# The groups of a latent attention, written out sixteen times or looped over two of four batches

## The chip, the cores and the metric

The kernel runs on one core of one Trainium2 chip. The metric is the device time of one execution in microseconds (us), the median of three. Its engines are TensorE (PE, with its weight loads shown as PEld), VectorE (DVE), ScalarE (ACT), GpSimd (POOL) and SyncE (SP, which issues nearly all DMAs here). Each runs its own instruction stream, and they meet only through semaphores.

## What is computed

Two attention layers and a mixture of experts, each with a norm ahead and behind. Only the middle part is touched by the change: an attention of 16 heads whose keys, queries and values have 4 numbers each, over 4 batches of 1024 tokens. Cut to that (B = 4, S = 1024, D = 128):

```python
# first layer: 16 causal heads of 64, tanh projections                    (block 1)
x = x + layernorm(attn_ref(layernorm(x), Wq, bq, Wk, bk, Wv, bv, Wo, bo))
hs = layernorm(x)
# second layer                                                            (block 2)
Q = (hs @ q_w + q_b)  -> [b, 16 heads, s, 8][..., :4]
K = (hs @ k_w + k_b)  -> [b, 16 heads, s, 4];  V = (hs @ v_w + v_b) -> the same
attn = softmax(einsum("bhsk,bhtk->bhst", Q, K) / sqrt(4))
mla_out = concat(einsum("bhst,bhtv->bhsv", attn, V), zeros) @ o_w + o_b
# router, top 2 of 8 experts, expert MLPs, weighted sum                   (block 3)
x = x + layernorm(hs + 0.3 * moe(mla_out))
```

## The kernel before

It is written per engine. Three large blocks follow one another, one for each part above, with a barrier between them. Numbers of the text such as "block 1" mean these.

**Block 1** goes over 32 pairs of heads. Its helper each_pair (lines 392 to 403) writes pairs 0 to 3 out in Python, loops with engine.Fori over pairs 4 to 9 and again over pairs 10 to 29, two pairs in each round, and writes the last two out. Line 396 is the first loop, line 399 the second. In a loop a wait's count is an expression of the loop's variable. **Block 3** loops over the experts in the same manner (line 1760 on TensorE).

**Block 2** is the one at issue. It goes over 16 groups: batch b (4) times gi (4), and a group is four heads of one batch. n = 4 b + gi is its number. A group is 32 items u: half h of the queries, key tile kt (8), pair pr of heads (2). In one item of a group

- TensorE makes the scores of 128 keys by 512 queries for two heads (L1086), then the same kind of product the other way round for a later item, "maxima" (L1116), from which the row maximum is taken 22 items ahead (LEAD), then some small piece of other work ("spare", L1152), and last the values product of two items before (L1101, 8 matmuls);
- ScalarE takes the exponential of the scores (L1293), 128 x 1024;
- VectorE reduces the maxima product to its maximum (L1467), 128 x 1024;
- GpSimd, twice a group, splits the found maxima into three bfloat16 parts (split_tops), which TensorE turns and VectorE puts into the rows of the next queries.

Scores and maxima take turns in three slots of PSUM (SLOT): scores of item u wait for the reduction of the slot's last user, maxima of item u wait for the exponential of item u - 1. Once a batch, at item 13 of gi 3, the order of the slots shifts, and maxima wait for one exponential more (SHIFT_AT, L1231).

In gi 0 and 1 of b 1 to 3 the outputs of the batch before are projected as well. In gi 2 of b 0 to 2 the next batch is prepared: its states are turned (L1067), queries, keys and values projected, split in three parts by GpSimd, and SyncE stores them to DRAM in 24 DMAs (store_part, L999). SyncE's eight loads for the next group (L1013) are issued at each group's start, when the scores of the group before have been issued to the end; TensorE needs them at item 10.

Semaphore counts are ITEMS * n + u + 1 and the like. at_least, prepares and is_first decide what is in a group; of a loop's variable they say "yes, beyond the first", "yes, prepares" and "no". wait_apart (L100) waits and then counts up a semaphore nobody waits for, so that the wait stays an instruction of its own. batch_tiles and the DMA helpers take a symbolic b through bass.ds. each_group (L978) runs group for all 16 on each of five engines, all written out: nothing in block 2 loops.

Of the kernel before, what the change touches and what calls it, by code (L numbers as in the profile page):

```python
# [23 lines left out]
B, S, D = 4, 1024, 128  # L24
# [10 lines left out]
GROUPS = H2 // GH  # L35
N2 = B * GROUPS
# [46 lines left out]
def build(nc, states, Wq, bq, Wk, bk, Wv, bv, Wo, bo, q_w, q_b, k_w, k_b, v_w, v_b, o_w, o_b,  # L83
# [7 lines left out]
    with ExitStack() as ctx:  # L91
# [885 lines left out]

        def each_group(engine, group):  # L978

            for n in range(N2):  # L980
                group(n // GROUPS, n % GROUPS, last=n == N2 - 1)

        def prepares(b):
            return not isinstance(b, int) or b < B - 1
# [1 line left out]
        with nc.Block() as block:  # L986
            @block.sync
            def _(sp):
# [69 lines left out]
                for c in range(PARTS):  # L1058
                    store_part(0, 1, c)
                sp.wait_ge(parts_out, 16 * STORES * 2)  # L1060
                each_group(sp, group)

            @block.tensor
            def _(pe):
# [196 lines left out]
                pe.wait_ge(lv_ready, 1)  # L1261
                turn_tops(0, 0)
                each_group(pe, group)
                values(N2 - 1, 1, ITEMS - 2)
                values(N2 - 1, 1, ITEMS - 1)
# [10 lines left out]
            def _(act):  # L1276
# [70 lines left out]
                for m in range(0, LEAD, 2):  # L1347
                    difference(m, SLOT[m % 3])
                each_group(act, group)
                copy_outputs(N2 - 1, 1)  # L1350
                copy_ao(B - 1, 1)
# [617 lines left out]
```

## Time and profile before

| | |
|---|---|
| three runs | 1759.78, 1766.03, 1773.70 us (median 1766.03) |
| profiled execution | 1773.7 us, span 1772.0 us |
| mean granted TensorE clock | 0.956 of full |
| busy | PE 93%, DVE 81%, ACT 69%, POOL 22% |
| block 1, its 32 pairs | about 50 to 800 us |
| block 2, its 16 groups | about 850 to 1543 us |
| block 3 | about 1545 to 1772 us |

The share of busy time is a mean over these blocks, which have different limits, so it is to be read block by block. Register, branch and semaphore instructions are not counted as busy; the trace has them all the same, as rows with a "q" behind the engine's name. PEclk is the clock that TensorE was granted, as a share of its upper level of 2.4 GHz; 0.5 is the lower level, 1.2 GHz.

### The profile page before, as it was taken

The numbers are of one execution on the slowest core, as the hardware profiler recorded it, in microseconds if no ns is written. First come the engines' busy times: TensorE is split into PE (matmuls) and PEld (weight loads), VectorE is DVE, ScalarE is ACT, GpSimd is POOL, SyncE is SP. The second block draws the span as 40 slices with busy tenths as digits, with TensorE's granted clock in tenths as the row PEclk, the third lists the DMA queues.
The fourth block names the chain that finished last, engine by engine and source line by source line (L and its number), as shares of the span: only waits on it lengthen the run. The fifth ranks groups of instructions, "written<-read, shape, count | busy, mean of one in ns | idle before, by whom it ended". The sixth has DMA issues, their size and how long they took to land. (4 is left out here: it accounts for less than half of the span.)

```text
span 1772.0 us, 38392 instructions
## 1 busy us (share of the span) xinstructions
PE 1640.3 (93%) x14930; PEld 713.5 (40%) x14930; DVE 1438.7 (81%) x2115; ACT 1218.5 (69%) x1185; POOL 384.8 (22%) x506
## 2 busy tenths in 40 slices
PE   2899999999999999985999999999999999889995
PEld 2344444444444444432223233323332332366774
DVE  5377777888888888887898899889989999277888
ACT  3666666666766666642787777777777778756776
POOL 6211112333333333323401000100010212120004
PEclk8999999999999999995899899989999999989998
DMA  4311001100000000002002000200020010000001
GB/s 136 74 48 39 37 37 38 38 37 36 37 37 37 37 26 31 20 4 59 26 26 48 13 13 25 48 14 13 26 48 14 13 37 13 10 6 13 13 12 48
DMA packets 48144, 57.02 MB, mean 32 GB/s; under 512 B 9406, under 2 KB 34462, under 8 KB 48032
## 3 DMA queue, kind: packets, MB, share of 16 engines
q1 hardware_dynamic: 46988, 53.71, 10.1%
q8 instruction: 77, 1.26, 0.3%
q10 hardware_dynamic: 1044, 1.76, 0.3%
q14 instruction: 35, 0.29, 0.1%
HBM read 15.07 MB, written 10.49 MB: 14 GB/s over the span
## 5 line engine op out<-in xcount | busy, mean ns | idle before, releaser
L1293 ACT ACTIVATE arena<-psum 128x1024 f32<-128x1024 f32 x512 | 522.9, 1024 | 152.3 <-PE psum L1086 138.2
L1467 DVE TENSOR_REDUCE arena<-psum 128x2 f32<-128x1024 f32 x490 | 581.4, 1220 | 56.1 <-PE psum L1116 53.0
L652 ACT ACTIVATE arena<-psum 128x2048 f32<-128x2048 f32 (+1 forms) x160 | 273.3, 1708 | 232.7 <-PE psum L537 229.9
L1101 PE MATMUL psum<-arena 128*32 128x256 f32 x4096 | 336.3, 401 | 1.1 <-ACT arena L1307 0.7
L554 PE MATMUL psum<-arena,hs 128*64 128x512 f32 (+3 forms) x1536 | 283.0, 496 | 2.7 <-POOL arena L701 2.2
L701 POOL TENSOR_SCALAR_AFFINE_SELECT arena<-arena 128x512 f32<-128x512 f32 (+1 forms) x160 | 168.0, 1068 | 533.9 <-ACT arena L652 533.9
L1116 PE MATMUL psum<-arena 32*128 32x512 bf16 x1068 | 211.6, 411 | 24.6 <-ACT arena L1346 11.8
L537 PE MATMUL psum<-arena 64*128 64x512 f16 (+3 forms) x2304 | 216.1, 325 | 4.9 <-DVE arena L738 3.6
L1086 PE MATMUL psum<-arena 32*128 32x512 bf16 x1024 | 203.3, 394 | 1.4 <-DVE arena L1489 1.4
L738 DVE TENSOR_TENSOR arena<-arena 128x1024 f16<-128x1024 f32 x64 | 78.4, 1225 | 138.5 <-ACT arena L631 138.5
L554 PEld LDWEIGHTS psum<-arena,hs 128*64 128x64 f32 x1536 | 96.1, 136 | 144.8 <-issue 125.9
L537 PEld LDWEIGHTS psum<-arena 64*128 64x128 f16 x2304 | 96.9, 94 | 137.7 <-issue 57.2
L1086 PEld LDWEIGHTS psum<-arena 32*128 32x128 bf16 x1024 | 48.2, 91 | 220.0 <-issue 135.1
L1101 PEld LDWEIGHTS psum<-arena 128*32 128x32 f32 x4096 | 82.4, 109 | 130.9 <-issue 115.4
L1782 ACT ACTIVATE arena<-psum,b1T 128x1024 f16<-128x1024 f32 x64 | 71.3, 1114 | 49.9 <-PE psum L1691 49.9
L1376 POOL CAST arena<-arena 128x16 bf16<-128x16 f32 x32 | 8.1, 254 | 428.7 <-DVE arena L1482 428.7
L1711 PE MATMUL psum<-arena 128*128 128x128 f16 x1536 | 94.0, 223 | 7.4 <-DVE arena L1624 4.2
L1116 PEld LDWEIGHTS psum<-arena 32*128 32x128 bf16 x1068 | 50.7, 94 | 120.8 <-ACT arena L1293 75.7
L502 PE MATMUL psum<-arena 128*128 128x512 f16 x384 | 95.3, 385 | 3.3 <-ACT arena L631 2.2
L1711 PEld LDWEIGHTS psum<-arena 128*128 128x128 f16 x1536 | 90.9, 100 | 15.6 <-issue 5.6
L1624 DVE TENSOR_TENSOR arena<-arena 128x1024 f16<-128x1024 f32 x60 | 73.1, 1223 | 27.6 <-ACT arena L1783 27.4
L1691 PE MATMUL psum<-arena 128*128 128x512 f16 x384 | 91.3, 389 | 2.2 <-ACT arena L1783 2.2
(202 smaller groups left out, 2122.8 us busy)
## 6 DMA issues: line engine op xcount, KB each, us to landing
arena<-arena SPq DMA_DIRECT2D x32, 512.0 KB, 3.0
arena<-arena SPq DMA_DIRECT2D x48, 128.0 KB, 2.3
arena<-latent_q SPq DMA_DIRECT2D x64, 64.0 KB, 2.0
arena<-latent_k SPq DMA_DIRECT2D x64, 64.0 KB, 2.0
arena<-arena SPq DMA_DIRECT2D x32, 96.0 KB, 2.6
X<-in_L_attn_states SPq DMA_DIRECT2D x4, 512.0 KB, 13.1
arena<-arena SPq DMA_DIRECT2D x32, 64.0 KB, 1.8
out_x<-X SPq DMA_DIRECT2D x4, 512.0 KB, 3.3
```

The lines of the kernel that those rows point to most:

```text
L502: last = nc.tensor.matmul(PJ[:, half * HALF:(half + 1) * HALF], w_qk[par][:, 2 * j + w, :], xT[par][:, x, half * HALF:(half + 1) * HALF], ...
L537: last = nc.tensor.matmul(SC[:, s, c:c + w], k[rows, kt * P:(kt + 1) * P], q[rows, q0:q0 + w], start=(m == 0), stop=(m == 2), skip_group_c ...
L554: last = nc.tensor.matmul(OUT[s * DH:(s + 1) * DH, q0:q0 + w], vals[par][:, kt, s * DH:(s + 1) * DH], probs[g][:, s, c:c + w], start=first ...
L652: nc.scalar.activation(probs[g], SC[:, :, 0:WIDTH[g]], ACT.Exp, scale=DH ** -0.5).then_inc(exp_done, 1)
L701: return nc.gpsimd.affine_select(out=v, in_=v, compare_op=ALU.is_ge, fill=0.0, base=0, pattern=[[0, blocks], [1, P]], channel_multiplier=-1)
L1086: last = nc.tensor.matmul(dst[:, i * HALF:(i + 1) * HALF], k_rows[par][rows, kt * P:(kt + 1) * P], q_rows[par][rows, h * HALF:(h + 1) * HA ...
L1101: last = nc.tensor.matmul(OT[ROWS * c:ROWS * (c + 1), h * HALF // 2:(h + 1) * HALF // 2], v_cols[par][:, kt, 2 * pr + i, :], e_probs[u % 4 ...
L1116: last = nc.tensor.matmul(dst[:, i * HALF:(i + 1) * HALF], q_rows[par][rows, qt * P:(qt + 1) * P], k[rows, :], start=(e == 0), stop=(e == ...
L1293: nc.scalar.activation(e_probs[u % 4], src, ACT.Exp, scale=KD ** -0.5).then_inc(e_done, 1)
L1467: nc.vector.tensor_reduce(half_tops[:, kh, qt, 2 * pr:2 * pr + 2], src.rearrange("p (i c) -> p i c", i=2), AX.X, ALU.max).then_inc(top_don ...
L1691: last = nc.tensor.matmul(HP[c][:, half * HALF:(half + 1) * HALF], w1_e[par][:, w, c * P:(c + 1) * P], mT[:, x, tok], start=(m == 0), stop ...
L1711: last = nc.tensor.matmul(YP[slot][:, tok], h[slot][c][:, tok], w2_e[par][:, w, c, :], start=(c == 0 and m == 0), stop=(c == FC - 1 and m ...
```

## The change

each_group no longer writes all 16 groups out. It writes the four groups of b 0 and of b 3 and loops over b 1 and 2 in between, with the four values of gi written out in the loop's body. The helpers are as they were; they had been written for a symbolic b already. Every engine's stream changes, since all five call each_group.

```diff
         def each_group(engine, group):
 
-            for n in range(N2):
-                group(n // GROUPS, n % GROUPS, last=n == N2 - 1)
+            for gi in range(GROUPS):
+                group(0, gi)
+            with engine.Fori(1, B - 1) as b:
+                for gi in range(GROUPS):
+                    group(b, gi)
+            for gi in range(GROUPS):
+                group(B - 1, gi, last=gi == GROUPS - 1)
```

## Rows read from the trace of the kernel before

**Rows 1.** The page: span, busy time and share, granted clock, the costliest VectorE group.

```profile
span 1772.0 us, 38392 instructions
PE 1640.3 (93%) x14930; PEld 713.5 (40%) x14930; DVE 1438.7 (81%) x2115; ACT 1218.5 (69%) x1185; POOL 384.8 (22%) x506
...
L1467 DVE TENSOR_REDUCE arena<-psum 128x2 f32<-128x1024 f32 x490 | 581.4, 1220 | 56.1 <-PE psum L1116 53.0
```

**Rows 2.** Windows by group: length, busy us of each engine, clock, DMA.

```profile
core 0: us, PE busy (x) PEld busy (x) DVE busy (x) ACT busy (x) POOL busy (x), PEclk, DMA share, GB/s
...
892.40:932.40 40.00, 39.60 (x400) 11.72 (x398) 38.96 (x41) 33.10 (x35) 2.42 (x10) 1.00 0.08 28
...
1157.70:1203.30 45.60, 44.14 (x398) 11.81 (x398) 39.24 (x41) 33.23 (x34) 2.42 (x10) 0.85 0.04 13
1203.30:1246.30 43.00, 41.62 (x414) 13.13 (x414) 40.23 (x42) 33.91 (x36) 2.43 (x10) 1.00 0.05 14
...
1335.40:1378.80 43.40, 41.93 (x398) 11.69 (x398) 39.21 (x41) 33.02 (x34) 2.42 (x10) 0.92 0.04 13
```

**Rows 3.** Timeline, seam of b 1 and b 2: start, length, engine, line.

```profile
1202.21 2.13 ACT L1293 ACTIVATE arena<-psum 128x1024 f32<-128x1024 f32 x2 [0.27 <-PE psum L1086]
...
1203.29 0.39 PE L1116 MATMUL psum<-arena 32*128 32x512 bf16 x2
```

**Rows 4.** Block 1: register work of line 651; pairs by L652; VectorE timeline.

```profile
L651 ACTq ALU_OP  x28: 35/35/38, 148.7 to 295.8; - x28
...
145.55:168.29 22.74, 8.55 (x6) 1.00 0.10 37
...
191.02:213.75 22.73, 8.55 (x5) 1.00 0.09 36
...
222.55 1.22 DVE L738 TENSOR_TENSOR arena<-arena 128x1024 f16<-128x1024 f32 x1 [2.34 <-ACT arena L631]
223.69 1.22 DVE L794 TENSOR_TENSOR arena<-arena 128x1024 f32<-128x1024 f32 x1
```

**Rows 5.** Block 3: line 1760, ns min/median/max; timeline after its branch.

```profile
L1760 PEldq COMPARE_BRANCH  x3: 79/222/222, 1662.3 to 1747.4; - x3
...
1663.17 0.80 PEld L1691 LDWEIGHTS psum<-arena 128*128 128x128 f16 x5
```

**Rows 6.** Windows: a round of block 1's loop, and batch b 1.

```profile
139.00:184.00 45.00, 45.00 (x392) 21.32 (x390) 34.14 (x41) 30.66 (x24) 7.43 (x11) 1.00 0.10 38
...
1025.60:1203.30 177.70, 171.12 (x1638) 52.12 (x1638) 159.29 (x164) 135.17 (x142) 16.10 (x44) 0.96 0.10 25
```

**Rows 7.** DMA queues, 340:740; 1025.6:1203.3; 852:1503 (issues: KB, us to landing).

```profile
q1 hardware_dynamic: 9792, 13.93, 9.3%
...
q8 instruction: 13, 0.21, 0.5%
...
latent_k<-arena SPq DMA_DIRECT2D x4, 32.0 KB, 1.9
...
arena<-in_L_ffn_w SPq DMA_DIRECT2D x1, 0.5 KB, 6.5
```

**Rows 8.** Timeline of TensorE at item 13, b 1, gi 3; the window behind it.

```profile
1175.25 0.39 PE L1116 MATMUL psum<-arena 32*128 32x512 bf16 x2 [1.12 <-ACT arena L1293]
...
1175.50:1189.20 13.70, 13.70 (x96) 2.93 (x94) 9.94 (x9) 7.53 (x8) 0.00 (x0) 0.50 0.00 0
```

**Rows 9.** Timeline of SyncE in gi 2 of b 1, and in block 1's loop.

```profile
1139.24 0.34 SPq L999 DMA_DIRECT2D latent_q<-arena  x1
...
1151.10 0.42 SPq L999 DMA_DIRECT2D latent_k<-arena  x1
1156.68 1.72 SPq L1013 DMA_DIRECT2D arena<-latent_q  x4
...
224.27 0.51 SPq L457 DMA_DIRECT2D arena<-arena  x1
224.96 0.51 SPq L459 DMA_DIRECT2D arena<-arena  x1
```

## The prediction

> **What bounds the kernel now.** I read the page first, then the same stage cut into windows, then one item of it in the timeline. On the page [rows 1] TensorE is busy for 93% of the span and VectorE for 81%, and the reduction of line 1467 is VectorE's largest group: 490 of them at 1.22 us. The change touches only the second block, the 16 groups b, gi from about 852 to 1543 us, so everything is decided there. Cut at the first exponential of each group [rows 2], a group of 32 items takes 40.0 us where nothing else is in it (b 0, gi 1), 43.0 us where the outputs of the batch before are turned and projected (b 2, gi 0), 45.6 us as gi 3 of b 1, 43.4 us as gi 3 of b 2. In the 40.0 us group VectorE is busy for 38.96 us, 97%; TensorE for 39.60 us. One item is 1.25 us, and the timeline of two [rows 3] shows a ring: two exponentials take 2.13 us, the maxima matmul of line 1116 starts at 1203.29, just as the first of them ends (1202.21 plus half of 2.13 is 1203.28), and the reduction follows it. So ScalarE, TensorE and VectorE hand over with under a tenth of a microsecond to spare: a cost of 0.1 us on every item would be seen, and a single stall is not made up, because VectorE's share of the first two is 97 and 94%.
>
> **What the change removes and adds.** It removes no engine instruction and moves none: the bodies for b 1 and 2 take the same branches for a symbolic b as for the numbers 1 and 2, with the same slots, waits and DMAs in the same order. It puts b 1 and 2 (groups 4 to 11, 32 x 8 = 256 items, 356 us) into a loop of two rounds on each of the five engines. Four things are new.
>
> First, wait counts must be computed. A count such as ITEMS * n + u + 1 is a constant now and becomes a register value. The first block shows that price, since its pairs 0 to 3 are written out and the later ones loop [rows 4]: in the loop the waits of line 651 show 28 register instructions of 35 ns. The pair written out before the loop's first lasts 22.74 us (145.55 to 168.29) and a pair in the loop 22.73 us: no difference. VectorE too: in the loop a reduction-sized operation at 222.55, 1.22 us long, is followed at 223.69 by one whose wait needs a register instruction; they overlap by 0.08 us as they do without one. So the sequencers do this work while the engine is busy. I take 0. The reason to doubt it is that the first block is held by TensorE alone at 100%, while here the ring is tight; the bound above is the whole register instruction on each item, 256 x 0.035 = 9 us, and worse if it sits behind the wait (a rival, below). The bound below is 0, since no instruction goes away from an engine's busy time.
>
> Second, the branch back, taken once by each engine (two rounds; entry and exit run on into the next code). In the third block's loop the TensorE branch takes 222 ns [rows 5] and starts 0.9 us before the next round's first weight load (1662.3 against 1663.17): that much work is still queued, and the branch costs nothing there. What differs here is the body's size. A round of the first block's loop is 392 matmuls and 390 weight loads, some 780 TensorE instructions; a round of the new loop is a batch, 1638 and 1638, some 3,280 [rows 6]. In 400 us of the first block's loop, more than eight rounds, the only queue with packets is q1: no instruction block is fetched at all, so 780 instructions stay in the engine's store. In the batch now, 13 blocks of 16 KB arrive on q8 [rows 7], one every 13.7 us, a stream just ahead of TensorE. After the branch back the first block of the body has to be there again. Whether it is, this trace does not show; 780 is held and 3,280 is four times that, so I take it as gone. The price is a fetch that nothing has started early. Bounds: 0.2 us, the branch alone, and 6.5 us, the slowest small load of the stage. Between them I take 3.0 us: 1.9 us, what the stage's 32 KB transfers need from issue to landing, plus 1.1 us for the one 16 KB packet (0.5% of 16 x 177.6 us over 13). With the branch's 0.2 us and less the 0.9 us still queued, TensorE stands still for 2.3 us.
>
> The Trainium skill, in Runtime: NRT & Kernel Launch, section Instruction fetch mechanics, says that instructions are prefetched in sequence only, that a store holds 2048 instructions on TensorE and 512 elsewhere, and that a taken branch out of what is held stalls for a DMA fetch, which is why it prefers full unrolling. The trace agrees as far as it goes: nothing is fetched again at 780. The page gives no duration for the stall; by its rule the same 3.0 us is paid, and by the rows' lower bound 0.2 us.
>
> The other engines branch under cover. VectorE's next reductions wait for TensorE anyway. ScalarE's body is about 290 instructions now and gains one register instruction per item; if its code must be fetched as well, that runs at the same time as TensorE's fetch, and ends with it. GpSimd has nothing due at the seam. I add nothing for them; uncovered they would cost up to another 3.0 us each.
>
> Third, what a standstill of TensorE sets off. In gi 3 of b 0, 1 and 2 line 1231 makes item 13 wait for one exponential more; TensorE idles 1.12 us until 1175.25 [rows 8], and from 1175.5 the granted clock is 0.50, the 1.2 GHz level, for 13.7 us, where 96 matmuls run in them. By the mean clock of the group [rows 2] the same place in b 2 gives 6.9 us (2 x 0.08 x 43.4), where b 1 gives 13.7 (2 x 0.15 x 45.6). The two groups are otherwise equal and last 45.6 and 43.4 us: 6.8 us less at the lower level is worth 2.2 us, so 13.7 us costs 4.4 us. The seam's 2.3 us is twice the idle after which the clock fell, so I expect one more such stretch: 3.3 us, midway. The bounds are 0 and 4.4.
>
> Fourth, the DMAs. SyncE issues 24 stores in gi 2 and 8 loads at the start of each group. With constant addresses the stores issue every 0.52 us (1139.24 to 1151.10 over 23), and the loads of gi 3 start at 1156.68 [rows 9]. In the first block's loop, with computed addresses, issues are 0.69 us apart (224.27, 224.96). 24 x 0.69 = 16.6 us from 1139.2 ends at 1155.8, the data at 1158; that delays the loads' start by 1.4 us, their 8 x 0.69 = 5.5 us end at 1163.6 and land by 1165.6. They are needed at item 10, over 12 us into a group that starts at 1157.7, so about 1170. The cover is 4 us; I count 0. Without it, the missing part would be paid twice, once a round.
>
> **The sum.** 0 (registers) + 2.3 (seam) + 3.3 (clock) + 0 (DMAs) = 5.6 us. The profiled execution took 1773.7 us (span 1772.0 and 1.7 around it), so 1779.3 by its own time; it was the slowest of three, 7.7 us over the median of 1766.0. On the median: 1771.6 us, 0.3% up.
>
> **The rivals.** (a) The registers are paid on every item. Where an instruction has two waits, the register instruction that computes the second count can carry the first wait, and the engine's own instruction comes behind it. If that befell the exponentials of line 1293, each would start later by at least 35 ns and a hand-over, 0.1 us together by the ring's own gaps [rows 3]; 256 x 0.1 = 26 us, 1797 us with the seam. For it: the ring is tight. Against: the count of its second wait, ITEMS * n + u - 3, is the number that the first wait used four items before, so it need not be computed again. (b) It is faster. The one mechanism I see is the clock: if the seam shifts the work against the moments at which the clock is granted, the stretches after line 1231 in b 1 and b 2 could vanish: 4.4 + 2.2 = 6.6 us, and a third of at most 4.4 in b 0. Net of the seam's 2.3 that is 1757 us; it decides only if TensorE does not idle at item 13, and nothing in the change alters that wait, so over 1% faster has little behind it. (c) The branch finds its code, or the queue covers it: no change, 1766 us. For it, every branch of this trace is free; against, the bodies are four times smaller. (d) The fetch is slow and each engine pays in turn: 6.5 + 3 x 3.0 + 4.4 = 20 us, 1786 us.
>
> **Chances.** Forecast (a seam of 2 to 10 us) 0.58; (c) 0.20; (a) 0.10; (d) 0.05; (b) in its small form 0.04; something unseen that gains more than 1%, 0.03. A difference under 1% (17.7 us) can hardly be told from none here: the three runs already lie 1759.8 to 1773.7. So same holds the forecast, (c), (b) and two of the five points of (d): 0.84; slower holds (a) and the rest of (d), 0.13; faster 0.03. The range is from 1760, the lowest run with a free seam, to 1784, the highest run plus 6.5 + 0.2 - 0.9 + 4.4 = 10.2 us. It leaves out (a), some of (d), (b) and the unseen gain, some 2 in 10.
>
> **What would show it.** Right: the groups of gi 0 keep 43.0 us but for the seam, and those of gi 3 stay at 43 to 46; between the last item of b 1 and the first of b 2 TensorE idles 2 to 3 us, with a q8 packet in the gap; the clock is at its lower level once more, right behind it; q8 and q14 have about as many packets in round two as in round one. Wrong: items in the loop longer than 1.25 us with ScalarE idle longer before line 1293 (then (a)); no gap at the seam (then (c)); loads of line 1013 landing after item 10; or the branches of several engines one behind another (then (d)).

## The result and the profile after

The changed kernel takes 1773.36 us (median of 12 runs, 1766.95 to 1783.92), the kernel before, measured beside it, 1764.77 us (12 runs, 1759.64 to 1773.70). The ratio is 1.0053, with a 95% interval of 1.0032 to 1.0076: 5.6 to 13.4 us slower, 8.6 by the medians. (A ratio is estimated from all runs of both kernels, here and below, and so it is not the quotient of the two medians.) The profiled execution took 1779.43 us. The page of after, the rows that answer to [rows 1] and the two queues of instruction blocks:

```profile
span 1777.6 us, 39595 instructions
PE 1640.0 (92%) x14930; PEld 715.8 (40%) x14930; DVE 1437.1 (81%) x2115; ACT 1218.6 (69%) x1185; POOL 384.3 (22%) x506
...
q8 instruction: 80, 1.31, 0.3%
...
q14 instruction: 42, 0.34, 0.1%
...
L1472 DVE TENSOR_REDUCE arena<-psum 128x2 f32<-128x1024 f32 x490 | 580.9, 1220 | 57.2 <-PE psum L1121 53.0
```

The work is the same: every engine's busy time is within 3 us of before. 1,203 more instructions are executed: 1,289 more of register work and branches, and 86 separate wait instructions less. q8 brings 80 blocks where it brought 77, q14 42 where it brought 35. (The lines of after are 5 higher behind the edit: L1086 became L1091, L1101 L1106, L1116 L1121, L1293 L1298, L1467 L1472.)

The windows by group, as in [rows 2]: the group of b 0 outside the loop, gi 0 of b 1, the two groups at the seam (gi 3 of b 1, gi 0 of b 2), gi 3 of b 2, and gi 0 of b 3 behind the loop:

```profile
core 0: us, PE busy (x) PEld busy (x) DVE busy (x) ACT busy (x) POOL busy (x), PEclk, DMA share, GB/s
894.70:934.60 39.90, 39.53 (x398) 11.67 (x398) 38.87 (x41) 33.06 (x35) 2.41 (x10) 1.00 0.09 28
...
1027.90:1071.20 43.30, 41.73 (x414) 13.16 (x412) 40.05 (x42) 33.84 (x37) 2.41 (x10) 1.00 0.05 14
...
1160.40:1204.60 44.20, 39.62 (x404) 11.80 (x405) 39.45 (x41) 33.23 (x34) 2.40 (x10) 1.00 0.07 20
1204.60:1252.00 47.40, 45.09 (x414) 13.35 (x411) 39.75 (x41) 34.09 (x36) 2.42 (x10) 0.89 0.03 8
1341.30:1382.50 41.20, 39.49 (x398) 11.74 (x396) 38.80 (x41) 33.16 (x35) 2.40 (x10) 1.00 0.05 15
...
1382.50:1425.50 43.00, 41.63 (x414) 13.14 (x412) 40.23 (x42) 33.93 (x37) 9.69 (x12) 1.00 0.05 14
```

The groups of the loop that hold neither the seam nor lowered clock are hardly longer than before, and the group behind the loop is back at 43.0. The two at the seam last 91.6 us together. Without the seam and at full clock they would take 84.2: gi 3 of b 2 shows what gi 3 lasts without lowered clock, 41.19, and gi 0 took 42.99 before. So the seam costs 7.4 us (91.57 less 84.18), 0.4 of it the registers of gi 0. The branches of the loop's line (count, ns min/median/max, first and last start):

```profile
L982 PEldq COMPARE_BRANCH  x2: 82/1735/3388, 1200.6 to 1381.5; - x2
...
L982 ACTq COMPARE_BRANCH  x2: 40/42/45, 1200.7 to 1381.6; - x2
...
L982 DVEq COMPARE_BRANCH  x2: 59/61/63, 1200.9 to 1381.8; - x2
```

TensorE's timeline over the seam (start, length, idle before it and what ended that):

```profile
1200.72 0.64 PE L1106 MATMUL psum<-arena 128*32 128x256 f32 x8
1204.23 0.39 PE L1091 MATMUL psum<-arena 32*128 32x512 bf16 x2 [2.87 <-issue]
...
1206.39 0.64 PE L1106 MATMUL psum<-arena 128*32 128x256 f32 x1
1207.76 1.08 PE L1106 MATMUL psum<-arena 128*32 128x256 f32 x7 [0.73 <-issue]
```

TensorE's branch back takes 3.39 us, against 82 ns for the same instruction when the loop is left. It starts at 1200.57 beside the last values product of b 1, and the first scores of b 2 wait for it for 2.87 us. A second standstill of 0.73 us follows at 1207.03, inside a values product whose matmuls wait for nothing. "<-issue" is how both look; no semaphore is named. In 1200 to 1211 us, by the DMA view, three 16 KB blocks start on q8 (1201.6, 1205.2, 1210.6) and four 8 KB blocks on q14:

```profile
q8 instruction: 3, 0.05, 1.9%
q14 instruction: 4, 0.03, 1.0%
```

The times of these packets tie both standstills to the fetch. The first block starts 1.04 us after the branch and has landed at 1202.60; the branch ends 1.36 us later. The second has landed at 1206.42, and the second standstill ends 1.34 us later. So the missing code is the cause of both, and the second comes about only where the second block is late: in the two profiles after_again and pe_alone of the next sections it lands 0.5 to 0.8 us earlier, counted from the branch's end (1.9 and 1.6 us behind it for 2.5), and there is no second standstill.

Behind the first standstill the clock is at its lower level for 10.2 us. The idle of item 13 ([rows 8]) is as long as before, by TensorE's timeline:

```profile
1178.11 0.39 PE L1121 MATMUL psum<-arena 32*128 32x512 bf16 x2 [1.12 <-ACT arena L1298]
```

But behind it the clock stays at full this time. The windows of 10.2 us behind either:

```profile
1204.80:1215.00 10.20, 9.47 (x60) 2.06 (x54) 6.09 (x5) 5.42 (x6) 0.41 (x2) 0.50 0.10 28
1178.20:1188.40 10.20, 10.04 (x100) 2.84 (x99) 9.66 (x9) 7.54 (x9) 0.00 (x0) 1.00 0.01 2
```

60 matmuls run in 10.2 us at the lower level, 100 in 10.2 us at the upper one. Half a clock doesn't mean half the speed of the stage: group gi 3 lasts 45.7, 43.5 and 41.2 us with 13.7, 6.8 and 0 us of lowered clock (b 1 and b 2 of before, b 2 of after), so a microsecond of it costs 0.33 us. The 10.2 us at the seam are 3.4 us.

One profile is one execution, but every recorded run has its span and its mean granted clock, and these give a second account. The spans of about a hundred runs of the kernel before lie on a line over the clock: 1766.0 us at 0.960, and 1.17 us more for each 0.001 less, with a scatter of 1.2 us around it. (0.001 of the mean clock is 3.5 us at the lower level, so this is again 0.33 us for each.) The 21 runs of the changed kernel lie 5.8 us above this line. That is what it costs at equal clock; the rest of the 8 us, 2.3 by the means, is more time at the lower level. Below, "at equal clock" is this height above the line; by the scatter, a mean of 10 or 12 runs is good to some 0.4 us.

### The profile page after: what moved, and what is told of

Read it like the earlier page. It is cut to its first block and busy times, and to the rows that moved or that the text cites. A ratio compares the mean times of both kernels' runs of the same rounds, so it can differ in the third digit from the quotient of the medians.

```text
span 1777.6 us, 39595 instructions
## 1 busy us (share of the span) xinstructions
PE 1640.0 (92%) x14930; PEld 715.8 (40%) x14930; DVE 1437.1 (81%) x2115; ACT 1218.6 (69%) x1185; POOL 384.3 (22%) x506
## 3 DMA queue, kind: packets, MB, share of 16 engines
q1 hardware_dynamic: 46988, 53.71, 10.2%
## 5 line engine op out<-in xcount | busy, mean ns | idle before, releaser
L1472 DVE TENSOR_REDUCE arena<-psum 128x2 f32<-128x1024 f32 x490 | 580.9, 1220 | 57.2 <-PE psum L1121 53.0
L1298 ACT ACTIVATE arena<-psum 128x1024 f32<-128x1024 f32 x512 | 522.7, 1024 | 151.9 <-PE psum L1091 137.5
L652 ACT ACTIVATE arena<-psum 128x2048 f32<-128x2048 f32 (+1 forms) x160 | 273.3, 1708 | 232.8 <-PE psum L537 230.0
L1106 PE MATMUL psum<-arena 128*32 128x256 f32 x4096 | 333.9, 398 | 2.5 <-issue 0.7
L1121 PE MATMUL psum<-arena 32*128 32x512 bf16 x1068 | 210.1, 408 | 24.7 <-ACT arena L1351 12.0
L1091 PE MATMUL psum<-arena 32*128 32x512 bf16 x1024 | 202.2, 392 | 4.4 <-issue 2.9
L1091 PEld LDWEIGHTS psum<-arena 32*128 32x128 bf16 x1024 | 48.3, 91 | 220.6 <-issue 129.1
L1106 PEld LDWEIGHTS psum<-arena 128*32 128x32 f32 x4096 | 82.2, 108 | 130.3 <-issue 114.4
L1121 PEld LDWEIGHTS psum<-arena 32*128 32x128 bf16 x1068 | 50.7, 93 | 121.9 <-ACT arena L1298 77.3
```

The source lines that it names most:

```text
L652: nc.scalar.activation(probs[g], SC[:, :, 0:WIDTH[g]], ACT.Exp, scale=DH ** -0.5).then_inc(exp_done, 1)
L1091: last = nc.tensor.matmul(dst[:, i * HALF:(i + 1) * HALF], k_rows[par][rows, kt * P:(kt + 1) * P], q_rows[par][rows, h * HALF:(h + 1) * HA ...
L1106: last = nc.tensor.matmul(OT[ROWS * c:ROWS * (c + 1), h * HALF // 2:(h + 1) * HALF // 2], v_cols[par][:, kt, 2 * pr + i, :], e_probs[u % 4 ...
L1121: last = nc.tensor.matmul(dst[:, i * HALF:(i + 1) * HALF], q_rows[par][rows, qt * P:(qt + 1) * P], k[rows, :], start=(e == 0), stop=(e == ...
L1298: nc.scalar.activation(e_probs[u % 4], src, ACT.Exp, scale=KD ** -0.5).then_inc(e_done, 1)
L1472: nc.vector.tensor_reduce(half_tops[:, kh, qt, 2 * pr:2 * pr + 2], src.rearrange("p (i c) -> p i c", i=2), AX.X, ALU.max).then_inc(top_don ...
```

## The experiments

All of them compute the full result. Lines move by some units from kernel to kernel; the texts say which operation a line is.

### The same kernel once more

> The changed kernel once more, beside the others of this batch. Theory (TensorE's branch back has to wait for its code, and TensorE's standstill then costs clock): 4 to 10 us over the kernel before, in the profile one TensorE branch of about 3.4 us at the seam of b 1 and b 2 and TensorE idle for 2.9 us. Rival (register work on every item): the groups of b 1 and b 2 are longer by more than 0.5 us each.

1776.67 us against 1767.46 beside it, ratio 1.0039 [1.0016, 1.0062], 4.8 us at equal clock. The groups of the loop are 0.36 us longer at most, so the rival is out. In its profile TensorE's branch takes 3.87 us, TensorE stands still for 3.35 us (1199.74 to 1203.09), and 10.2 us of lowered clock follow at once. The seam is no accident of one execution.

### Which engine's branch costs it

```diff
 def each_group(engine, group):
+    if engine.engine != mybir.EngineType.PE:      # pe_alone; act_alone and dve_alone with ScalarE,
+        for n in range(N2):                       # VectorE for TensorE; pe_out with == PE
+            group(n // GROUPS, n % GROUPS, last=n == N2 - 1)
+        return
     for gi in range(GROUPS):
         group(0, gi)
```

> Only TensorE loops over b 1 and 2; the other four engines stay written out. Theory: the whole seam is TensorE's, so the time is that of the changed kernel within 1.5 us, branch 3.4 us, TensorE idle 2.9 us. Rival (ScalarE's or VectorE's branch or register work carries it): half of the difference or less is left, under 4 us over before.

> The other way round: TensorE's groups are written out, the other four engines loop. Theory: no standstill of TensorE at the seam over 0.5 us and at most 1.5 us over the kernel before: only the register work of ScalarE and VectorE, seen as 0.15 us on a group and 0.36 us on the first of a round. Rival (the other engines' branches cost as well): 3 us or more over before, with a gap of 1 us or more at the seam.

> Only ScalarE runs batches 1 and 2 in a loop, the other four engines are written out; full computation. Theory (ScalarE's cold fetch): TensorE idles about 1.6 us at the seam, waiting for the exponential, as when all engines but TensorE loop; 8 KB instruction blocks arrive in the gap. Rival (it was VectorE's fetch): no idle over 0.3 us of TensorE at the seam here.

> Only VectorE runs batches 1 and 2 in a loop, the other four engines are written out; full computation. Theory (the 1.6 us are ScalarE's): no idle of TensorE over 0.3 us at the seam, and the time within 1 us of before. Rival (VectorE's fetch does it): about 1.6 us of idle there, ended by a wait for VectorE or for the exponential behind it.

| kernel | who loops | us, before beside it | ratio, 95% | at equal clock | idle of TensorE at the seam | lower clock behind it |
|---|---|---|---|---|---|---|
| after | all | 1773.4, 1764.8 | 1.0053 [1.0032, 1.0076] | 5.8 | 2.87 + 0.73 | 10.2 |
| after_again | all | 1776.7, 1767.5 | 1.0039 [1.0016, 1.0062] | 4.8 | 3.35 | 10.2 |
| pe_alone | TensorE | 1773.7, 1767.5 | 1.0036 [1.0013, 1.0059] | 3.4 | 2.84 | 17.1 |
| pe_out | all but TensorE | 1770.9, 1767.5 | 1.0014 [0.9992, 1.0036] | 2.4 | 1.66 | 3.4 |
| act_alone | ScalarE | 1769.8, 1766.5 | 1.0021 [1.0003, 1.0039] | 3.2 | 1.74 | 3.4 |
| dve_alone | VectorE | 1773.4, 1766.5 | 1.0023 [1.0002, 1.0045] | 2.7 | 1.46 | 10.2 |

In the last four L1095 is the scores, L1125 the maxima. TensorE's timeline at the seam in pe_alone:

```profile
1200.31 0.39 PE L1095 MATMUL psum<-arena 32*128 32x512 bf16 x2 [2.84 <-issue]
```

In pe_out:

```profile
1202.10 0.39 PE L1125 MATMUL psum<-arena 32*128 32x512 bf16 x2 [1.66 <-ACT arena L1302]
```

In act_alone:

```profile
1197.60 0.39 PE L1125 MATMUL psum<-arena 32*128 32x512 bf16 x2 [1.74 <-ACT arena L1302]
```

In dve_alone:

```profile
1201.88 0.39 PE L1095 MATMUL psum<-arena 32*128 32x512 bf16 x2 [1.46 <-DVE arena L1476]
```

TensorE's own branch leaves the mark of the changed kernel: idle ended by issue. But each of the other two computing engines costs TensorE 1.5 to 1.7 us when it loops alone, and the reader sees it as a plain wait: for the exponential (L1302) or for the reduction (L1476). The late engine itself, ScalarE in act_alone and VectorE in dve_alone:

```profile
1196.52 1.94 ACT L1302 ACTIVATE arena<-psum 128x1024 f32<-128x1024 f32 x2 [1.99 <-PE psum L1095]
...
1200.60 3.49 DVE L1476 TENSOR_REDUCE arena<-psum 128x2 f32<-128x1024 f32 x3 [1.68 <-PE psum L1125]
```

Their branches take 45 and 63 ns; what is late is the code behind them. ScalarE's exponential starts 1.95 us after its scores have ended, where 0.04 us is usual, and VectorE's reduction 0.75 us after its matmul, where 0.04 is usual too. In act_alone no instruction at all stands on ScalarE for 2.72 us behind the branch, not even a register instruction, which waits for nobody. Two 8 KB blocks start on q14 in each case: at 1194.5 and 1197.3 in act_alone, at 1198.6 and 1201.1 in dve_alone.

Three expectations failed here. For dve_alone I had expected no idle over 0.3 us; VectorE's fetch is nearly as dear as ScalarE's. For pe_out I had expected no idle over 0.5 us, and found 1.66. And pe_alone was to lie within 1.5 us of the changed kernel; at equal clock it lies 1.4 us under after_again, its neighbour in time, and 2.4 under after, so the other four engines are not for nothing.

Alone they leave 2.84, 1.74 and 1.46 us, 6.0 us in sum, and all together, in after, 3.6. ScalarE's and VectorE's, 1.74 and 1.46, leave 1.66 together in pe_out. So the fetches run side by side, and the longest hides most of the others. That is also why making four engines' code straight (pe_alone) gains only 1.4 to 2.4 us at equal clock, of which the register work is about 1.3.

### Is it the missing code, and can it be had earlier

```diff
-            with engine.Fori(1, B - 1) as b:
+            with nc.Fori(1, B - 1, engines=OrderedEngineSet([engine.engine]),
+                         hint_back_edge=True) as b:      # hint_pe: on TensorE alone; hint_two: TensorE, ScalarE
```

> The changed kernel with every engine announcing its branch back, so that the first instructions of the body can be fetched before the branch is taken; full computation. Theory (what is left at the seam when only TensorE announces it, 1.59 us of idle before the maxima, is ScalarE's own fetch): each branch takes 0.4 us or less, TensorE idles less than 0.5 us at the seam, no lower clock right behind it, and the time is within 2 us of before, what the register work of the loop costs. Rival (the 1.6 us come from something else, as the register waits of the first items): an idle of about 1.6 us before the maxima stays, with 3 us more than before in all.

> The changed kernel with TensorE and ScalarE announcing their branches back, VectorE, GpSimd and SyncE not; full computation. When all five announced it, the seam was clear but behind the loop's end two new stalls came: 0.35 us at item 14 of the first group behind the loop (b 3, gi 0) and 1.5 us at items 12 to 14 of the next, the second followed by 10.2 us of lower clock; there VectorE starts a reduction 0.55 us after its matmul has ended. Theory A (an engine that announced its branch has fetched the start of the body again when the loop ends, and runs into code behind it that is not there yet; the late one is VectorE): the two stalls are gone, groups b 3 gi 0 and gi 1 are back at 43.0 and 41.5 us, but at the seam TensorE idles about 1.5 us for VectorE's cold fetch, as when VectorE alone loops. Theory B (the stalls behind the loop are TensorE's or ScalarE's, or no matter of the announcement): they stay. In time: A about 4 us over before, B about 9.

TensorE's branches in hint_pe:

```profile
L983 PEldq COMPARE_BRANCH  x2: 93/236/378, 1202.0 to 1378.5; - x2
```

Its timeline at the seam of hint_pe (L1123 maxima, L1300 exponential):

```profile
1205.95 0.39 PE L1123 MATMUL psum<-arena 32*128 32x512 bf16 x2 [1.59 <-ACT arena L1300]
```

Announced, TensorE's branch takes 0.38 us for 3.39, and its standstill is gone; what stood behind it comes up, 1.59 us of waiting for ScalarE's late exponential, with 3.4 us of lower clock behind it. I had expected under 0.5 us and no lower clock. The time is 1772.19 us, ratio 1.0019 [0.9993, 1.0045], 3.4 us at equal clock. When all five announce it (hint_all), TensorE idles at most 0.42 us at the seam, with no lower clock behind it: the seam's cost is nearly gone. Yet the time is 1776.48 us beside 1766.50, ratio 1.0053 [1.0032, 1.0074], and I had expected 2 us at most. The loss is behind the loop. The timeline of hint_all in gi 1 of b 3, items 12 to 14 (L1474 reduction, L1123 maxima, L1093 scores, L1154 spare):

```profile
1436.52 0.39 PE L1123 MATMUL psum<-arena 32*128 32x512 bf16 x2
...
1437.46 3.49 DVE L1474 TENSOR_REDUCE arena<-psum 128x2 f32<-128x1024 f32 x3 [1.57 <-PE psum L1123]
...
1438.74 0.39 PE L1093 MATMUL psum<-arena 32*128 32x512 bf16 x2 [0.94 <-DVE arena L1474]
...
1441.33 0.48 PE L1154 MATMUL psum<-arena 64*128 64x128 f32 x2 [0.69 <-DVE arena L1496]
```

The maxima matmul has ended at 1436.91, but the reduction starts at 1437.46, 0.55 us behind it for the usual 0.04. A block on q14 has landed at 1436.12, 1.34 us ahead of the reduction, the same delay as from block to code at TensorE's seam; the next block starts behind it (1438.1). TensorE idles 0.9 and 0.7 us in consequence, and 10.2 us of lowered clock follow from 1443.2: the group lasts 46.44 us where before it lasted 41.50. The group ahead of it has another 0.35 us at item 14. With some 1.4 us of registers and 0.7 us left at the seam, these are 7.4 us of the 10.0 between the medians; what the rest is stays open. The profile of before and those of after and hint_pe show nothing there.

hint_two, without VectorE's announcement, takes 1769.01 us beside 1767.80, ratio 1.0023 [1.0001, 1.0046]. The large stall is gone in its profile (gi 1 of b 3 lasts 41.50 us), a smaller one of 0.5 us stays in gi 0 of b 3 (43.53), and at the seam TensorE idles 0.53 and 0.70 us, the second one for VectorE, 1.2 us in all where 1.5 had been expected; no lower clock in the loop at all in this profile. ScalarE's timeline in hint_two at the smaller stall:

```profile
1395.26 1.94 ACT L1300 ACTIVATE arena<-psum 128x1024 f32<-128x1024 f32 x2 [1.65 <-PE psum L1093]
```

Its scores ended at 1394.69, so this exponential starts 0.57 us late; in hint_pe, where TensorE alone announces its branch, the same group lasts 42.98 us and has no such stall. So the small stall comes with ScalarE's announcement. The large one belongs to VectorE's, as theory A has it, by one profile of either kernel only: at equal clock hint_all and hint_two both lie 4.4 us above before, and the many runs do not show what leaving out VectorE's announcement gains. None of the three beats the kernel before, and their intervals overlap with that of the changed kernel. That an announced engine has its store full of the loop's start when it leaves the loop would explain both stalls; that part is argued, and no run separates it.

### The size of the body

The first block of the kernel before has a loop on TensorE of ten rounds with two pairs each. Two kernels put more pairs into a round, on TensorE alone, and a third announces the branch:

```diff
-            with engine.Fori(NORM_FROM // 2, N1 // 2 - 1) as k:
-                for par in range(2):
-                    pair(2 * k + par, par, norm=True)
+            step = 5 if engine.engine == mybir.EngineType.PE else 1      # pairs_ten; 2 in pairs_four
+            with engine.Fori(NORM_FROM // 2, N1 // 2 - 1, step) as k:    # four_hint: 2, and hint_back_edge
+                for m in range(step):
+                    for par in range(2):
+                        pair(2 * (k + m) + par, par, norm=True)
```

> The kernel before, block 2 written out, but in block 1 TensorE loops over pairs 10 to 29 in two rounds of ten pairs instead of ten rounds of two: about 3,900 TensorE instructions a round instead of 780. Theory (a body beyond what the engine's store holds has to be fetched again): the one taken branch of line 399 takes about 3.4 us instead of 0.21, TensorE, busy 100% there, stands still for 2 to 3 us, and the time is 2 to 3 us over before, up to 4.4 us more if the clock falls. Rival (the seam of block 2 is special): the branch stays at 0.2 us and the time is that of before.

> The same with five rounds of four pairs, about 1,560 TensorE instructions a round. Theory by what block 3 shows (a body of 960 matmuls and weight loads branches free): the rows do not say whether 1,560 fit. The Trainium skill (Runtime: NRT & Kernel Launch, section Instruction fetch mechanics) says that 2048 fit on TensorE; by that rule every branch stays near 0.2 us. If they fit, the time is that of before within 1 us and the four branches take 0.2 us each; if not, four branches of 3.4 us make it 9 us or more over before.

> The kernel before with its first block as in the run of 5 rounds of 4 pairs on TensorE (four taken branches of 3.3 to 3.9 us, 28.3 us over before), but TensorE announces its branch back; full computation. Theory (the price is a fetch that nothing starts early, and the announcement starts it): the four branches take under 0.5 us each, no idle over 0.5 us behind them, and the time is within 3 us of before. Rival (the loop is dear because its code does not fit and is streamed anew each round, whatever is announced): idles of 2 us and more stay at the four branches, 20 us or more over before.

| kernel | TensorE instructions in a round | branches taken, ns | q8 blocks in 340 to 740 us | ratio, 95% |
|---|---|---|---|---|
| before | 780 | 208 (median of 9) | 0 | 1 |
| pairs_four | 1,560 | 3939, 3741, 3347, 3808 | 36 | 1.0164 [1.0135, 1.0194] |
| pairs_ten | 3,900 | 3562 | 29 | 1.0043 [1.0024, 1.0063] |
| four_hint | 1,560 | 249, 228, 223, 223 | 2 | 0.9987 [0.9969, 1.0004] |

TensorE's branches in pairs_four:

```profile
L400 PEldq COMPARE_BRANCH  x5: 83/3741/3939, 373.7 to 772.2; - x5
```

Its timeline behind the first of them (L539 and L556 are attention products of block 1):

```profile
373.77 1.25 PE L539 MATMUL psum<-arena 64*128 64x512 f16 x16
377.79 1.07 PE L556 MATMUL psum<-arena,hs 128*64 128x256 f32 x6 [2.77 <-issue]
380.67 1.11 PE L556 MATMUL psum<-arena,hs 128*64 128x256 f32 x2 [1.81 <-issue]
```

TensorE's branches in four_hint:

```profile
L401 PEldq COMPARE_BRANCH  x5: 87/223/249, 375.6 to 745.3; - x5
```

Nothing of block 2 is in this: a long body makes the branch cold by itself. 29.9 us by the medians over four cold branches are 7.5 us each, in a block that TensorE alone bounds; the one of pairs_ten is 8.5. By the profiles the loop of pairs_four is 28.8 us longer than that of before, 7.2 for each branch, that of pairs_ten 7.4 and that of four_hint 0.1. Each of the five has two standstills (2.2 to 2.8 us, then 1.4 to 2.4) and 3.4 to 6.8 us of lowered clock. What I had not expected is the pair pairs_four and four_hint. They have the same round; with the branch announced the two blocks arrive in the first round (340.8, 356.3) and none in the four behind it, so the 1,560 instructions (1,646 with registers and waits) do fit into the store. The Trainium skill gives 2048 for TensorE (Runtime: NRT & Kernel Launch, section Instruction fetch mechanics), and four_hint agrees; without the announcement the trace shows that a body below that number is fetched anew in every round, 36 blocks in 400 us. Fetching in sequence past the branch, over the start of the body, would do this, and the counts speak for it: each round of pairs_four that begins with a cold branch takes 9 blocks, while the 4,112 instructions of the second round of pairs_ten take 18, so the 1,646 of a round are 7 blocks at most, and about two are fetched beyond them. What these two hold is not shown.

### The price of a handover in the ring

```diff
 def exp(n, u, src):
-    act.wait_ge(sc_done, ITEMS * n + u + 1)
     upto(act, ov_done, ITEMS * n + u - 3)
+    wait_apart(act, sc_done, ITEMS * n + u + 1)
     nc.scalar.activation(e_probs[u % 4], src, ACT.Exp, scale=KD ** -0.5).then_inc(e_done, 1)
```

> The kernel before, written out, but in block 2 each of the 512 exponentials stands behind a separate wait instruction for its scores, which is where a register instruction carrying the wait would put it. The prediction's rival (a) priced this at 0.1 us an item, and called the ring of engines tight. If the ring is tight: 512 x 0.1 = 51 us over before, 2.9%. If the ring has slack of a tenth in most groups: under 15 us over before, with VectorE's share of the 40 us groups unchanged.

1782.66 us beside 1765.88, ratio 1.0098 [1.0065, 1.0131]: 16.8 us over 512 items, 0.033 us each. It lies between the two expectations, just above the slack one's 15 us. The window of the group of [rows 2] that took 40.0 us:

```profile
890.20:931.30 41.10, 39.58 (x398) 11.69 (x396) 39.42 (x41) 33.04 (x35) 2.41 (x10) 1.00 0.08 27
```

Before, the exponential carries the wait for its scores itself; here a separate instruction does. That lengthens the group by 1.1 us of 40. It gives each item less than the 0.1 us of the expectation: the exponentials that have to wait start 0.116 us behind their scores (the median), where they start 0.042 us behind them before. Of these 0.074 us the ring passes on 0.033, a little under half.

## Why the prediction was right, and where its terms were off

The time (1771.6 predicted, 1773.4 measured, range 1760 to 1784) and the mechanism hold: the registers cost little, the branch back of TensorE is cold, the clock falls behind it, once. The range alone says little, since it holds "no change" (1766) too; it is the standstill in the profile that tells the forecast from rival (c). The sum was 5.6 us and the profile's accounts give 8.4, close to the medians' 8.6; their part without the clock, 5.0, is what the runs show at equal clock (5.8 and 4.8).

| term | predicted | measured | how |
|---|---|---|---|
| registers | 0 (0 to 9) | 1.4 | groups of the loop at full clock against before |
| standstill | 2.3 (0.2 to 6.5) | 3.6 | 2.87 + 0.73, after |
| clock | 3.3 (0 to 4.4) | 3.4 | 10.2 us at 0.33 us each |
| DMAs | 0 | 0 | gi 3 of b 2 lasts 41.2 us |

**The registers.** The step holds nearly: gi 0 of b 1 lasts 43.35 us for 42.99, gi 1 and 2 0.15 us more than before, gi 3 under 0.1. Not one item in general is longer; the difference sits in three to six items of a group, at 0.03 to 0.1 us each. 124 of 128 exponentials of a round have a register instruction, as the row of their wait's line shows, and most of them cost nothing:

```profile
L1296 ACTq ALU_OP  x248: 35/35/38, 1027.8 to 1380.3; - x124
```

pe_alone, where only TensorE computes its counts, shows 0.09 us in gi 2 and nothing in gi 0, 1 and 3; the rest is the other engines'. Rival (a) is out, at 26 us. The exponentials of the loop that have to wait start 0.041 us behind their scores, 0.042 before, all but the first two of each group: there the register instruction does carry the wait for the scores, and they start 0.12 us behind them. So the rival's mechanism exists, at two items of 32, and takes 0.08 us of each group. Its price was wrong too: it put 0.1 us on every item down whole, and by exp_apart a little under half of a delay is passed on.

**The seam.** Found cold, as taken. The size failed in two places. For the first standstill 1.9 + 1.1 + 0.2 - 0.9 = 2.3 was counted against 2.87; the branch took 3.39 us where 3.2 was counted, and only 0.5 us of it was hidden where 0.9 was. That 3.2 came so near is in part luck. Only the packet was put together from its own row (1.1 for 0.99 measured); the rest, 2.1 from a data transfer, is 1.04 us ahead of the packet and 1.36 behind it. The second, 0.73 us, was not in the sum at all: behind the first block the next has to come too, and the stream that ran ahead of TensorE starts with no lead. The larger one in pairs_four (1.81) shows the same; after_again and pe_alone have none.

**"The other engines branch under cover"** is the step that was wrong as it was worded. It named two covers, VectorE's waiting for TensorE and a fetch at the same time as TensorE's. The first is none: VectorE's code is late for its own reasons, and alone it costs 1.46 us. The second holds and carries the sum: 6.0 us apart are 3.6 together. Rival (d), each engine in turn, is out for the same reason; its price for an engine laid bare, up to 3.0 us, was measured as 1.5 to 1.7. "I add nothing for them" came out nearly right only because TensorE's own fetch was the longest.

**The clock.** The size is right for this profile. In the nine profiles in which TensorE stood still for 1.46 us or more at a cold branch, the lower level followed each time, for 3.4 to 17.1 us. Behind the 1.12 us of item 13 it followed in some profiles and not in others, with the same work around it. Rival (b) named just this, that those stretches could vanish; in the profile of after they did, in b 1 and b 2, and saved it 6.8 us against the profile of before. It was put aside with a wrong condition, that this needs an item 13 at which TensorE does not idle: it idled 1.12 us and the stretches vanished all the same. One sign of being right failed with it, gi 3 of b 2 lasting 41.2 us and not 43 to 46. That is why block 2 is only 1.6 us longer in the profile of after, 8.4 less 6.8; the other 4.1 of the 5.7 us between the two spans lie ahead of block 2 (2.2) and behind it (1.9). It is the scatter of single executions and no effect of the change: pairs_ten and pairs_four, whose block 2 is that of before, show 6.8 us of the lower level in gi 3 of b 1 and none in b 2, four_hint none and 3.4, where the profile of before had 13.7 and 6.8. The medians of many runs do not show a gain.

**The DMAs.** SyncE's stores in the loop issue 0.61 us apart (1142.21 to 1156.25 over 23) where 0.69 was counted, and the loads of gi 3 start at 1159.70, 0.8 us ahead of the group, before 1.0. Nothing waits for them. (The groups 4 to 11 last 353 us before, not the 356 of the prediction; nothing hangs on it.)

Rival (c), a branch that finds its code, is out: it is what four_hint shows and after does not.

## What to carry to other kernels

In these kernels a loop's branch back is free while the body stays in the engine's store. Where it does not, TensorE's costs some 7 us each time by the profiles (7.0 in block 2, 7.2 and 7.4 in block 1), as stall and as lowered clock. So before looping over long code, count the instructions of the body on each engine and the taken branches, and look on the instruction queues for whether code is fetched in rounds that should hold it; announcing the branch can bring the price down to nothing (four_hint), but must be timed, since it can move the stall to the code behind the loop (hint_all). An engine whose cold branch is hidden is hidden only behind the longest of the others: taking that one away uncovers the next.

## What the runs showed of the hardware that was not expected

- The same 1,560 instructions on TensorE are fetched anew in each round with an ordinary branch (36 blocks of 16 KB in 400 us, 3.3 to 3.9 us for each branch) and stay in place with an announced one (2 blocks, 0.22 to 0.25 us).
- VectorE and ScalarE fetch in blocks of 8 KB on q14, and a cold branch shows there not in the branch (45 and 63 ns) but as an idle of the engine behind it, put down to a semaphore that had long been given (1.95 us in act_alone, 0.75 in dve_alone).
- Code is executed about 1.35 us after its block has landed (1.36 and 1.34 us at the seam of after). A cold branch of TensorE can have a second standstill, from 3.1 us behind the branch's end on at the seam: 0.7 to 2.4 us in after, pairs_four and pairs_ten, none in after_again and pe_alone, where the second block lands earlier.
- At equal clock the changed kernel is 5 to 6 us slower; a microsecond at the lower level costs 0.33 us, in block 2 by three groups of one kind and over the whole kernel by a hundred runs of before.
